# Decays of two scan layers: sums broadcast by DMA and subtracted in the exponential's bias, instead of a matrix product of split rows

## The reference

```python
G = jnp.cumsum(gc, axis=-1)                                   # attention, 32 heads
scores = jnp.einsum('bhnid,bhnjd->bhnij', qc, kc)
decay = jnp.where(causal, jnp.exp(G[..., :, None] - G[..., None, :]), 0.0)
y_intra = jnp.einsum('bhnij,bhnjd->bhnid', scores * decay, xc)

A_cum = jnp.cumsum(A_dt, axis=-1)                             # mixer, 128 heads, 8 groups
L = jnp.exp(_segsum(A_dt))                                    # exp(A_i - A_j), 0 above the diagonal
Y_diag = jnp.einsum('bzlhn,bzshn,bhzls,bzshp->bzlhp', Cc, Bc, L, xch)
decay_states = jnp.exp(A_cum[..., -1:] - A_cum)
```

## Time and profile before

| | |
|---|---|
| time before, 3 runs | 2699.6, 2704.6, 2707.73 us; median 2704.6 |
| the profiled execution's own time | 2708.85 us |
| its span (first to last instruction) | 2707.1 us |
| mean granted TensorE clock | 0.979 |
| DMA | 118.79 MB, mean 44 GB/s |

### The profile page before, as it was taken

How to read it: one execution, slowest core, us unless ns; L and a number is a source line. 1 busy time by engine, 2 the same in 40 slices (tenths; PEclk the granted TensorE clock), 3 DMA queues, 4 the chain that set the end, 5 groups by cost and what they waited for, 6 DMA issues and landing times.

```text
span 2707.1 us, 58907 instructions
## 1 busy us (share of the span) xinstructions
PE 2567.5 (95%) x19678; PEld 2045.6 (76%) x19678; DVE 1862.9 (69%) x2720; ACT 1363.2 (50%) x2492; POOL 1428.0 (53%) x1404
## 2 busy tenths in 40 slices
PE   4999999999999759899999999999999999999989
PEld 3778787787787538677787787777777877877777
DVE  5675766666757568757677767587576777685864
ACT  3434434334334345656665665665566656656621
POOL 1654655546546110457556656475575566564720
PEclk8999999999999769999999999999999999999999
DMA  2010110110110014211111111101111111111011
GB/s 90 24 50 26 35 44 23 44 40 19 52 36 12 17 59 140 78 45 38 50 33 58 34 41 50 38 30 50 45 38 50 33 58 34 42 49 38 19 46 47
DMA packets 72632, 118.79 MB, mean 44 GB/s; under 512 B 10310, under 2 KB 22214, under 8 KB 72373
## 3 DMA queue, kind: packets, MB, share of 16 engines
q1 hardware_dynamic: 72388, 115.61, 13.1%
HBM read 102.92 MB, written 12.65 MB: 43 GB/s over the span
## 4 chain that ended last, share of the span: by engine, by line
PE 52%; DVE 3%; issue 2%; POOL 2%; ACT 0%; DVEq 0%; POOLq 0%; ACTq 0%
PE proj L218 11%; PE proj L220 11%; PE proj L219 11%; PE core_y L1409 5%; PE core_o L1415 2%; PE decay L1471 1%; PE turned L253 1%; DVE mx_acc L1216 1%; PE turned L1439 1%; PE mx_decay L1471 1%; PE mx_normed L1439 1%; PE mx_normed L253 1%; PE core_y L220 1%; PE core_y L218 1%; PE mx_decay L220 1%
## 5 line engine op out<-in xcount | busy, mean ns | idle before, releaser
L218 PE MATMUL proj<-slab_hi,XTL 128*128 128x512 f32 x816 | 355.3, 435 | 0.0
L201 DVE TENSOR_TENSOR slab_lo<-slab_raw,slab_hi 128x512 fp32r<-128x512 f32 (+2 forms) x272 | 245.5, 915 | 148.7 <-ACT slab_hi L192 123.1
L218 PE MATMUL proj<-XTH,slab_lo 128*128 128x512 f32 x736 | 301.2, 409 | 41.0 <-PEq L81 14.4
L220 PE MATMUL proj<-slab_hi,XTH 128*128 128x512 f32 x816 | 321.1, 393 | 0.0
L219 PE MATMUL proj<-slab_lo,XTH 128*128 128x512 f32 x816 | 318.7, 391 | 0.0
L219 PE MATMUL proj<-XTL,slab_hi 128*128 128x512 f32 x736 | 292.9, 398 | 0.0
L220 PE MATMUL proj<-XTH,slab_hi 128*128 128x512 f32 x736 | 292.9, 398 | 0.0
L1670 POOL TENSOR_TENSOR mx_th<-mx_th,mx_acc 128x512 f32<-128x512 f32 x48 | 62.2, 1296 | 363.4 <-ACT mx_th L1569 363.4
L1687 POOL TENSOR_TENSOR mx_gate<-mx_gate,mx_hd 128x512 f32<-128x512 f32 x128 | 167.9, 1312 | 152.1 <-DVE mx_hd L1601 141.1
L218 PE MATMUL proj<-slab_hi,mx_otl 128*128 128x512 f32 x576 | 242.0, 420 | 4.1 <-DVE mx_otl L267 4.1
L220 PE MATMUL proj<-slab_hi,mx_oth 128*128 128x512 f32 x576 | 227.8, 396 | 0.0
(11 more groups left out here) (358 smaller groups left out, 6667.4 us busy)
## 6 DMA issues: line engine op xcount, KB each, us to landing
slab_raw<-in_w_gate SPq DMA_DIRECT2D x64, 256.0 KB, 3.0
slab_raw<-in_w_out SPq DMA_DIRECT2D x64, 256.0 KB, 3.0
slab_raw<-in_w_x SPq DMA_DIRECT2D x60, 256.0 KB, 3.6
slab_raw<-in_w_q SPq DMA_DIRECT2D x32, 256.0 KB, 3.0
slab_raw<-in_w_g SPq DMA_DIRECT2D x32, 256.0 KB, 3.0
slab_raw<-in_w_o SPq DMA_DIRECT2D x32, 256.0 KB, 2.9
bc_scratch<-bc_acc SPq DMA_DIRECT2D x32, 256.0 KB, 2.0
slab_raw<-in_w_bc SPq DMA_DIRECT2D x20, 256.0 KB, 4.4
```

The source lines that it names most:

```text
L201: op = nc.vector.tensor_tensor(K.SL[par][:, c, 0:width], K.RAW[c][:, 0:width], hi, ALU.subtract)
L218: nc.tensor.matmul(to[:, 0:bh.shape[-1]], al, bh, start=(c == 0), stop=False)
L220: mm = nc.tensor.matmul(to[:, 0:bh.shape[-1]], ah, bh, start=False, stop=(c == KC - 1))
```

## The change

1. The decay products go, with their split rows, their constants and their loads. Instead SP loads whole tiles in which all 128 partitions hold the same row G_i: in the attention 12 loads of 256 KB a round into `at_g_all`, in the mixer one load of 512 KB for each tile (8 a half) into a ring of four, `mx_g_all`, each from a row of DRAM read 128 times.
2. GpSimd writes -3e38 above the diagonal of these tiles (an affine select on 128x1024, list `CUT`): 4 a round in the attention, in place of the 8 selects on 128x512 at line 961; 8 a half in the mixer, where there were none, and where the multiplication with the triangle on VectorE becomes a copy.
3. ScalarE computes exp(G_i + bias) with the bias -G_j of each partition (`less`), or G_last - G_j (`left`), so it does one head (128x128) at a time: 4 instead of 1 or 2 instructions in a pair of the attention, 8 instead of 4 in a tile of the mixer. In the mixer it writes into the two PSUM banks that held the decay products.
4. `decay_phase` stores G alone, and turns G and G_last - G_j by PE; in the mixer's case over two banks, with the exponential on the way out.
5. The attention turns its tiles and v in two banks (`TB`, the freed decay bank is one), as the mixer does.

```diff
@@ attention_phase
+    CUT = [-2, 1, 4, 7]
+        TB = [K.PT, K.PD]
-        PD = [K.PD, mem.enter_context(nc.psum_tensor("at_decay", [P, SLAB], F32))]
+        GB = [sb(f"g_all{b}", [P, 3, REP0, P]) for b in range(NB)]
 # SP
-                sp.wait_ge(S["at_set"], HEAD + 1)
-                sp.wait_ge(K.unit_done, HEAD + U + SLOTS * g)
-                sp.dma_start(RHS[0:3, :, :, :], rd[:, :, ds(REP0 * g, REP0), :]).then_inc(S["at_rows"], 16)
...
+                sp.wait_ge(S["at_e"], HEAD + PAIRS * g)
+                for b in range(NB):
+                    for k, it in enumerate((0, 1, 1)):
+                        src = sums[b, it:it + 1, ds(REP0 * P * g, REP0 * P)].broadcast_to([P, REP0 * P])
+                        sp.dma_start(GB[b][:, k, :, :].rearrange("p h n -> p (h n)"), src).then_inc(S["at_rows"], 16)
 # PE
-                nc.tensor.matmul(PD[k % 2][:, :], LHS[:, int(p == 1), jt * P:(jt + 1) * P], RHS[...],
-                                 start=True, stop=True).then_inc(S["at_pair"], 1)
...
 # product
-                pe.wait_ge(S["at_mask"], HEAD + NT * g + t + 1)
+                pe.wait_ge(S["at_m"], HEAD + PAIRS * g + 3 * b + (3 if t % 2 else 1))
 # ACT
-                                nc.scalar.activation(ex, PD[k % 2][:, :], ACT.Relu, scale=-1.0).then_inc(S["at_rl"], 1)
-                                nc.scalar.activation(ex, ex, ACT.Exp, scale=-1.0).then_inc(S["at_e"], 1)
+                            act.wait_ge(S["at_cut"], HEAD + NB * g + b + 1)
+                            for h in range(REP0):
+                                ex = nc.scalar.activation(EX[k % 2][:, h, :], GB[b][:, block_of, h, :], ACT.Exp,
+                                                          bias=(left if p == 1 else less)[:, jt, ds(REP0 * g + h, 1)])
 # POOL
+                        diag = GB[b][:, 0:2, :, :].rearrange("p c h n -> p (c h) n")
+                        nc.gpsimd.affine_select(out=diag, in_=diag, ..., fill=NEG, ...).then_inc(S["at_cut"], 1)
-                            nc.gpsimd.affine_select(out=mk, in_=mk, ..., fill=0.0, ...).then_inc(S["at_mask"], 1)

@@ mixer_phase
+    CUT = {0: (0, 1, 2, 3), OFF + 4: (4,), OFF + 6: (5,), OFF + 7: (6,), OFF + 8: (7,)}
+        GB = [sb(f"g_all{i}", [P, HH1, P]) for i in range(4)]
 # SP: before the first group row_load(0, 0..3), then in each half
+            def row_load(q, t):
+                sp.wait_ge(S["mx_e"], HEAD + 16 * q + 2 * t - 6)
+                sp.dma_start(GB[t % 4][:, :, :]..., sums[t:t + 1, ds(HH1 * P * q, HH1 * P)]
+                             .broadcast_to([P, HH1 * P])).then_inc(S[f"mx_row{t % 4}"], 16)
...
                     slab(q, 2)
-                    row_loads(q, 2)
-                    row_loads(q, 3)
+                    for t in range(4, NT):
+                        row_load(q, t)
...
                         slab(q, 3)
+                        for t in range(4):
+                            row_load(q + 1, t)
 # PE
-                            nc.tensor.matmul(PD[k][:, :], LHS[b % 2][:, k, cols], RHS[b % 2][:, 4 * k:4 * k + 4, cols],
-                                             start=True, stop=True).then_inc(S["mx_d"], 1)
 # ACT
+                        act.wait_ge(S["mx_cut"], HEAD + NT * q + t + 1)
                         for k in range(2):
-                            nc.scalar.activation(PD[k][:, :], PD[k][:, :], ACT.Relu, scale=-1.0).then_inc(S["mx_rl"], 1)
-                            nc.scalar.activation(PD[k][:, :], PD[k][:, :], ACT.Exp, scale=-1.0).then_inc(S["mx_e"], 1)
+                            act.wait_ge(S["mx_m"], HEAD + 16 * q + 2 * t + k - 1)
+                            for h in range(4):
+                                ex = nc.scalar.activation(PD[k][:, h * P:(h + 1) * P], GB[t % 4][:, 4 * k + h, :], ACT.Exp,
+                                                          bias=less[:, t, ds(HH1 * q + 4 * k + h, 1)])
 # DVE, s == 0, slots 4 and 6
-                        nc.vector.tensor_tensor(CBM[...], K.PO[...], tri[...], ALU.mult)
+                        nc.vector.tensor_copy(CBM[...], K.PO[:, :])
 # POOL
+                    for t in CUT.get(sl, ()):
+                        pool.wait_ge(S[f"mx_row{t % 4}"], HEAD + 32 * q + 16 * (t // 4 + 1))
+                        nc.gpsimd.affine_select(out=GB[t % 4][:, :, :], in_=GB[t % 4][:, :, :], ..., fill=NEG, ...)
```

277 lines of the change are left out of this document (98 added, 179 removed).

## The result

The changed kernel takes 2716.5 us (median of 13 runs, 2709.9 to 2721.5). The kernel before takes 2705.7 us on the same chips (13 runs). The ratio is 1.0036, with a 95% interval of 1.0026 to 1.0046. So it is slower by about 10 us, where 2636 us had been forecast. The prediction was wrong in size and in sign.

The account below looks back on a forecast made before the run. PE was taken to bound both layers. Mixer 41.5 + attention 22.1 + decay phases 10 - DMA 3 = 70.6 us off 2708.85 gives 2638, off the median 2704.6 gives 2634; stated 2636, range 2600 to 2682.

Parts of the forecast that it names:

- SP has no other work that waits behind them for longer than the slabs are early: DMA term, SP's queue: the new broadcast loads (88 MB of new loads against 118.8) delay no later load harmfully.
- Nothing lost; PE's 22.1 us are kept whole: Attention, GpSimd: four selects of 1.08 us replace eight of 0.634, 0.8 us less, so PE's whole gain remains.
- PE's price of a decay product: PE: a pair costs 0.43 us in the mixer, one product 0.23 us in the attention; 77 us together.
- ScalarE: Exponentials of 128 columns at 0.29 us each, 2.3 us a mixer tile, the same as before; counted as 0.
- GpSimd in the mixer: Selects of 1.08 us; odd halves gain 1.75 us of 3.44, even halves keep all 3.44; mixer 41.5 us.
- The decay phases: Before the layers' products: attention's phase 3 us shorter, mixer's 5 us; together 10 us gained, 5 to 14.
- The start of the mixer: Ahead of the mixer's first group, four 512 KB loads precede B and C: 3 us lost once (0 to 7).
- the fourth, a slow broadcast: Mixer loads reading the same 4 KB 128 times are slow; at 40 GB/s 390 us more in all; chance 0.03.
- landing more than 10 us after its issue: Sign set for the slow-broadcast rival: `mx_g_all` in the mixer landing that late would show the forecast wrong.
- The rival of a slower kernel, ScalarE: Mixer slots 16 to 18: exponentials of 0.55 us make ScalarE the bound, 88 us more, 2722 us; chance 0.07.

## Why the prediction was wrong, step by step

- **The step that failed: "SP has no other work that waits behind them for longer than the slabs are early".** The slabs of w_g do. The rate was at hand: 512 KB in 3.7 us is 142 GB/s, so 3 MB ahead of w_g are 22 us. I checked the sum of bytes against the time of a half and a tile's load against its four slots, all in the mixer, and priced the order on the queue only once, ahead of the mixer's first group. The attention's twelve loads in one burst were not looked at. Their place ahead of w_g cost 67 us, the difference between the changed kernel and the one with w_g first. By the profiles, which are 60 us apart, it is 13.2 us up to the first round's product and 7.0 us in each later round: PE stands still for 6.6 us a round instead of 1.6, and the other 2.0 us are matmuls at half clock behind the stall, a cost that the prediction has no term for.
- **"Nothing lost; PE's 22.1 us are kept whole", in the attention:** right for GpSimd, wrong as a whole. The rounds were 3.3 to 6.0 us longer. With the order mended they are 2.8 shorter.
- **PE's price of a decay product** was right in the attention: 2.76 us a round forecast, 2.8 found. In the mixer the pair's 0.43 us is found at the 48 tiles where the product with B and C stands ahead of it (from the product's start to the unit's fourth matmul 3.12 us before and 2.69 after, medians), and 0.34 us at the 48 where it doesn't (2.17 and 1.83). The row that the 0.43 was read from has no product ahead of the pair. That is 4 us too much in the sum.
- **ScalarE:** 0.29 us an exponential was right; two groups of four take 1.17 us each from start to start:

```profile
1626.69 1.24 ACT L1473 ACTIVATE decay<-mx_g_all,less_sum 128x128 f32<-128x128 f32 x4
1627.86 1.23 ACT L1473 ACTIVATE mx_decay<-mx_g_all,less_sum 128x128 f32<-128x128 f32 x4
1629.03 0.58 ACT L1490 ACTIVATE mx_gate<-proj 128x512 f32<-128x512 f32 x1
```

- **GpSimd in the mixer:** the select's 1.08 us was right (1.09, the median), and so was the picture: between tiles 1 and 7 no idle time but the 0.16 to 0.45 us between its own dependent operations, and PE waiting for `mx_xch`. The size was not. The mixer gave 18.4 us of 41.5. The intervals from odd to even gave 0.2 us each instead of 1.8, and those from even to odd, which were to keep all 3.4, gave 1.9 (721.1 to 705.8 us over eight). Of the 1.5 us missing there 0.8 are new waits of PE, for VectorE's sum `mx_hd` and for the SiLU of the next half; 0.3 are the smaller price of a pair (below 0.43 at three of eight), and the rest was not traced. I counted the gaps up to tile 3 and the lateness at the last product, and took a place among GpSimd's instructions for a fixed distance to PE. That each delay passes from one to the other and back would explain it, but no run separates this. The selects account for 8 us of it by the medians as the kernel was and for 8 to 14 with the better order, and the order of xch and gate for some 10, of which 4 are there in the kernel before too.
- **The decay phases:** the mixer's was 5.4 us shorter (5 forecast: from the first turned tile to the next projection 11.8 us before, 6.4 now). The attention's start came at 43.19 us instead of 45.06, 1.9 of the 3 forecast.
- **The start of the mixer** was priced at 3 us lost (0 to 7); it lost 8.5, the slab behind 2 MB again. With the slab first PE still waits 4.9 us there, behind the four selects, where it was 1.2 before.
- **Rivals:** the fourth, a slow broadcast, was nearest to what happened, but it was put as a matter of the sum of bytes, in the mixer. There a broadcast lands in 3.7 us. Its sign, "landing more than 10 us after its issue", was set for `mx_g_all`; it was `at_g_all` that took 9.5, and the slab behind it. The rival of a slower kernel, ScalarE, had nothing to do with it.

The version to keep is the changed one with three edits of order: both slabs ahead of the broadcasts, and the product's input first on GpSimd. It takes 2631 to 2636 us, 2.6 to 2.8% less than the kernel before. That this is the 2636 of the forecast is chance: the attention gives more than forecast, the mixer less, and the order on GpSimd is worth some 4 us without the change.

## What to carry to other kernels

When small loads become large ones, list what is issued behind them on the same queue, divide the bytes ahead by the rate that a row of the trace gives, and compare that with how early each of these loads was; do so for every burst, not for the sum. A stall of TensorE can cost more than its length, so look at the granted clock of the stretch behind it. A late slab doesn't stall its own reader alone: what stands behind the split on an in-order engine is late too, and the profile names that. An engine without a gap can be a bound whatever its share of busy time says, and then the order of its own instructions can be worth as much as their number: here some 10 us, against 8 to 14 for the selects.

## What the runs showed of the hardware

The engines moved far less in the attention's burst than at the mixer's start. The windows (last two columns: share of the DMA engines' time, GB/s), the first with broadcasts of 2 KB a partition, the second with broadcasts of 4 KB a partition and slabs together:

```profile
272.00:292.00 20.00, 20.00 (x93) 16.44 (x92) 9.01 (x12) 4.66 (x8) 6.00 (x4) 1.00 0.78 160
```

```profile
1117.00:1131.00 14.00, 11.67 (x47) 9.20 (x45) 0.45 (x1) 2.39 (x3) 4.38 (x4) 0.92 0.94 289
```

The Trainium skill, "DMA: Bandwidth & Descriptors", section "Bandwidth", gives 341 GB/s for a load of 1 MB issued by GpSimd. Neither stretch here, issued by SP, reaches it. Whether the row length makes the difference was not tried.

An issue on SP also gets slower once some broadcasts are outstanding. In the burst that starts at 271.83 us the first four take 0.33 to 0.38 us each, from the fifth on 0.71 to 1.57. With broadcasts of 512 and 256 KB in turn, in the same round, it is the fourth that takes 0.95 us, and the next take 1.2 to 1.6.

The start of a matmul behind the product with B and C is no safe mark. After the change the unit's second matmul starts 0.63 us after the first, where 0.23 us is usual, which looks as if the decay products had hidden something. From the product with B and C to the unit's second matmul it is 1.63 us before (first two rows) and 1.19 after (last two), 0.44 less, which is the forecast price of the pair:

```profile
1534.24 1.13 PE L1415 MATMUL core_o<-mx_xd,mx_CBO 128*128 128x512 f32 x2
1535.87 0.40 PE L219 MATMUL proj<-slab_lo,XTH 128*128 128x512 f32 x1
```

```profile
1556.53 1.13 PE L1355 MATMUL core_o<-mx_xd,mx_CBO 128*128 128x512 f32 x2
1557.72 0.40 PE L215 MATMUL proj<-slab_lo,XTH 128*128 128x512 f32 x1
```
